# Four moves in the TensorE order of a fused attention and FFN kernel, and one move on ScalarE

## The chip, the cores and the metric

The kernel runs on one core of a Trainium2 chip. The metric is device time in microseconds (us) for one execution, the median of several. The core has five engines that run side by side and meet only at semaphores: TensorE (PE in the profile, its weight loads PEld), VectorE (DVE), ScalarE (ACT), GpSimd (POOL) and SyncE (SP), which here issues the DMAs.

## The reference

For each of 8 batches of 128 tokens and 512 features the program computes an attention block and an FFN block, each with a residual.

```python
c  = x @ cond_weight[id1].T                  # a weight chosen per batch
q, k, v = c @ Wq, c @ Wk, c @ Wv             # 32 query heads, 8 key/value groups, head size 16
q, k = rope(q), rope(k)
w  = softmax(causal(q k^T) / 4)
x1 = x + (w v) @ Wo
h  = x1 @ W.T + 0.5 * (x1 @ lora_A[id2]) @ lora_B.T
out = x1 + h @ W_base.T + b_base + 2 * sum_top2( gate_e * (h @ A_e^T) @ B_e^T )   # router: h @ W_router.T
```

## The kernel before

**Tiling.** A batch is one tile of 128 tokens. All fp32 products are made from two rounded parts ("hi" and "lo"): `with_high` adds hi times hi and lo times hi for the four slices of 128 features (8 matmuls), `with_low` the four others. ScalarE makes a hi part (a copy), VectorE the lo part (a difference), so a product over a fresh tile waits first for ScalarE and then for VectorE. The FFN's weights are fused ahead of the loop: `fused_w` holds W times [router, experts' A, W_base], cut into a left block (`HALF` = 324 columns: 8 router logits, 128 expert values, 188 base columns) and a right block. The rank part (x1 times lora_A, rank 32) is `project_low`, four matmuls into `d_ps`; `split_low` on ScalarE and VectorE makes `low_t` from it, and one matmul with `lora_g` (line 1141, "the last product") adds it to a block.

**Rounds.** The work is a software pipeline. Round t (1 to 6) holds batch f = t + 1 (condition, q, k, v, first scores), batch t (maxima, transposed scores, exponentials), batch r = t - 1 (context, output projection, x1, FFN) and batch q = t - 2 (experts, output). Before the rounds stands a prologue, behind them a tail that finishes batches 6 and 7.

**What sets the order.** Each engine's order is written out by hand as a list of calls, and each engine executes its list in order. Nothing is reordered by a scheduler; a wait at the head of the list holds everything behind it on that engine.

**The steps that matter here, by engine:**
- TensorE: `transpose_maxima` (line 1013) turns the row maxima of batch t; `score_t(t, e)` makes the transposed scores of one half e: 16 mask products of 32x32 (line 1025, "the mask"), 12 products (line 1030, "the passes"), 4 that subtract the maxima (line 1035). `project_out` (lines 976, 977, 981) makes the attention output of batch r. `transpose_qk` (lines 1096 and 987) turns q and k of batch f; `transpose_x1` (line 987) turns x1; `project_low` (line 1126); `project_ffn` (lines 976, 977, 981, then 1141); `score(f, 0)` and `score(f, 1)` (line 1003). The last product of the left block signals `gates_done`.
- ScalarE: `copy_v` (v out of PSUM), `spread_maxima` (four copies into `max_rows`), `split_context`, `exp_scores` (line 519), `split_qk`, `split_x1`, `split_low`.
- VectorE: `choose_experts` starts on `gates_done` (line 794), then `add_x_base`, `maxima` 0, `gate_hidden`, `maxima` 1, `turn_context` (line 703), `split_hidden`, `split_c` (line 622, `c_t_lo`), `maxima` 2 and 3, `split_maxima`, context scaling, `add_out`, the rotations (lines 735, 737), `split_context`, `add_x` (line 775) and the lo parts.
- GpSimd: `add_rotated` (line 374) makes the rotated k and q for `transpose_qk`; `split_a` (line 369).

Of the kernel before, what the change touches and what calls it, by code (L numbers as in the profile page):

```python
# [19 lines left out]
def build_program(nc, x, x_t, cond_ids, lora_ids, cond_w_t, w_q, w_kv, w_o, cos, sin, w2, lora_a, lora_b,  # L20
# [34 lines left out]
    with ExitStack() as ctx:  # L55
# [361 lines left out]
        def _(act):  # L417
# [78 lines left out]
            def copy_v(f):  # L496
                act.wait_ge(kv_done, f + 1)
                if f == 0:
                    act.wait_ge(zeroed, 9)
                v = d_ps[:, KV:2 * KV].rearrange("s (j e d) -> s j e d", e=2, d=HD)  # L500
                for e in range(2):
                    copy(v_ones[f % 2][e][:, :, 0, :], v[:, :, e, :]).then_inc(v_ready, 1)
# [67 lines left out]
            for t in ROUNDS:  # L570
# [10 lines left out]
                if prep:  # L581
                    split_condition(g, range(KT))
                    split_xt(g)
                if batch(f):
                    copy_v(f)
                if batch(t):
# [3 lines left out]
                if batch(t):  # L590
                    exp_scores(t, 0)
                if batch(f):
                    split_qk(f)
                if batch(r):
# [25 lines left out]
        def _(dve):  # L620
# [352 lines left out]
        def _(pe):  # L973
# [41 lines left out]

            def score_t(t, e):
                if e == 0:
                    pe.wait_ge(maxed, HEADS * (t + 1))
                    if t == 0:
                        pe.wait_ge(owns_made, 7)  # L1020
                for j in range(PAIRS):
                    if e == 1:
                        pe.wait_ge(exped, 8 * t + j + 1)
                    for b in range(PAIRS):
                        nc.tensor.matmul(s_ps[j][tile_rows(b), :], ident_b[tile_rows(j), tile_rows(j)],
                                         later_b[tile_rows(j), b, :].unsqueeze(1).broadcast_to([TILE, PER, P]),
                                         start=True, stop=False)
                for key, query in passes(k_pad[t % 2], q_t[t % 2]):
                    for j in range(PAIRS):
                        nc.tensor.matmul(s_ps[j][:, :], key[tile_rows(j), e, :], query[tile_rows(j), :, :],  # L1030
                                         start=False, stop=False)
                if e == 0:
                    pe.wait_ge(max_spread, t + 1)
# [53 lines left out]

            def project_kv(f):
                if f > 1:
                    pe.wait_ge(ctx_turned, 2 * (f - 1))  # L1090
                with_high(d_ps[:, 0:2 * KV], c_t, qkv_w, slice(D, QKV))
                with_low(d_ps[:, 0:2 * KV], c_t, qkv_w, slice(D, QKV)).then_inc(kv_done, 1)
# [6 lines left out]
            def project_out(r):  # L1099
                pe.wait_ge(o_lo, KT)  # L1100
                pe.wait_ge(ctx_hi, r + 1)
# [4 lines left out]
                elif r > 0:  # L1106
                    pe.wait_ge(out_ready, r)
                with_high(attn_ps(r)[:, :], ctx_t, o_w, slice(0, D))
                pe.wait_ge(ctx_lo, r + 1)
                with_low(attn_ps(r)[:, :], ctx_t, o_w, slice(0, D)).then_inc(attn_done, 1)  # L1110
# [18 lines left out]

            def project_ffn(r, n, to, part=slice(0, HALF)):  # L1130
                cols = slice(n * HALF + part.start, n * HALF + part.stop)
                if r == 0:
# [3 lines left out]
                if n == 0 and r == LAST - 1:  # L1136
                    pe.wait_ge(ctx_turned, 2 * r + 3)
                with_high(to[:, part], x1_t, fused_w, cols)
                with_low(to[:, part], x1_t, fused_w, cols, last=False)
                pe.wait_ge(low_lo, r + 1)  # L1140
                return nc.tensor.matmul(to[:, part], low_t, lora_g[:, cols], start=False, stop=(n == 0))

            def transpose_hidden(q):
# [73 lines left out]
            for t in ROUNDS:  # L1217
# [20 lines left out]
                if batch(f):  # L1238
                    project_kv(f)
                if batch(t):  # L1240
                    transpose_maxima(t)
                    score_t(t, 0)
# [92 lines left out]
```

## Time and profile before

| | |
|---|---|
| median of 3 runs | 255.9 us (255.59 to 256.31) |
| profiled execution, device time | 255.72 us |
| its span in the profile | 253.9 us |
| TensorE busy | 228.1 us (90%) |
| VectorE busy | 182.6 us (72%) |
| ScalarE busy | 117.3 us (46%) |
| GpSimd busy | 86.5 us (34%) |

The span runs from the first to the last instruction; 1.8 us of the execution lie outside it. A matmul's end in the profile is modelled and overlaps the next one's start, so TensorE is read by the starts of its rows: two full rows of 512 columns start 0.23 us apart. TensorE's granted clock is full in nearly all slices.

### The profile page before, as it was taken

Reading aid. Unit: us, or ns where it says so; the run is one execution under the profiler, and the core shown is the slowest. Engines: PE = TensorE matmul, PEld = TensorE weight load, DVE = VectorE, ACT = ScalarE, POOL = GpSimd, SP = SyncE. Lnnn points to the kernel's source line nnn. Section 1 sums busy time; section 2 is a strip of 40 time slices with the busy share of each in tenths; the row PEclk is TensorE's granted clock in tenths of the full one; section 3 lists DMA queues with packets and bytes.
Section 4 is the critical chain, followed back from the end, with each engine's and each line's share of the span. In section 5 each row is a group of like instructions: output and inputs, shape, how many; then the busy total and the mean of one; then the engine's idle time right before and its main releaser. Section 6 shows DMA issues by size and latency. Waiting matters only on the chain.

```text
span 253.9 us, 5663 instructions
## 1 busy us (share of the span) xinstructions
PE 228.1 (90%) x1978; PEld 169.9 (67%) x1978; DVE 182.6 (72%) x915; ACT 117.3 (46%) x269; POOL 86.5 (34%) x93
## 2 busy tenths in 40 slices
PE   0588999989999999999999998999999998989894
PEld 0477977765667676777667766867775764656793
DVE  3499367638966896599749974988488947967753
ACT  3596436477374237514661566066602461054210
POOL 7200562359178006900490039202930140002020
PEclk9999999999999999999999999999999999999998
DMA  5999208015002401250116011601100120001111
GB/s 118 335 381 366 98 7 252 4 27 183 12 5 79 170 1 52 54 196 4 52 44 206 4 53 41 209 1 54 41 3 0 45 52 0 3 1 55 41 41 41
DMA packets 20047, 21.16 MB, mean 83 GB/s; under 512 B 6452, under 2 KB 11572, under 8 KB 20020
## 3 DMA queue, kind: packets, MB, share of 16 engines
q1 hardware_dynamic: 20020, 20.81, 25.3%
q8 instruction: 15, 0.25, 0.4%
q14 instruction: 12, 0.10, 0.1%
HBM read 18.71 MB, written 2.10 MB: 82 GB/s over the span
## 4 chain that ended last, share of the span: by engine, by line
PE 66%; DVE 16%; ACT 11%; issue 3%; DMA 1%; SPq 1%; POOL 1%; DVEq 0%
PE bank L976 10%; PE bank L981 9%; PE bank L977 9%; ACT stage_d L519 5%; PE bank L1055 5%; PE bank L1003 4%; PE bank L1069 3%; PE bank L987 3%; PE bank L1030 3%; DVE thrown L685 3%; PE bank L1071 3%; PE bank L1070 3%; ACT max_rows L419 2%; PE bank L1035 2%; DVE x L775 2%
## 5 line engine op out<-in xcount | busy, mean ns | idle before, releaser
L685 DVE CUSTOM_DVE_ANT_0 thrown<-bank,causal 128x128 f32<-128x128 f32 x256 | 56.1, 285 | 0.0
L374 POOL TENSOR_TENSOR rope_b<-rope_a,rope_b 128x128 f32<-128x128 f32 (+1 forms) x16 | 16.3, 1016 | 94.5 <-DVE rope_b L737 94.5
L354 POOL TENSOR_TENSOR cond_w_lo<-cond_raw,cond_w_hi 128x512 fp32r<-128x512 f32 x28 | 35.2, 1287 | 23.9 <-ACT cond_w_hi L419 23.9
L1069 PE MATMUL bank<-cond_w_hi,xt_hi 128*128 128x512 f32 x32 | 13.6, 425 | 9.4 <-DVE cond_w_lo L622 9.4
L976 PE MATMUL bank<-qkv_w_hi,c_t_hi 128*128 128x512 f32 (+1 forms) x64 | 21.4, 352 | 0.6 <-DVE c_t_lo L622 0.5
L685 DVE DVE_READ_ACCUMULATOR2_ANT neg_max<- 128x1 f32 x256 | 21.0, 82 | 0.0
L976 PE MATMUL bank<-fused_w_hi,late 128*128 128x324 f32 (+2 forms) x68 | 20.5, 316 | 0.0
L977 PE MATMUL bank<-qkv_w_lo,c_t_hi 128*128 128x512 f32 (+1 forms) x64 | 20.5, 337 | 0.0
L383 POOL TENSOR_TENSOR x_bias<-x,bias_row 128x512 f32<-128x512 f32 x8 | 10.2, 1277 | 29.9 <-DVE out_sb L843 28.8
L977 PE MATMUL bank<-fused_w_lo,late 128*128 128x324 f32 (+2 forms) x68 | 19.9, 306 | 0.0
L419 ACT ACTIVATE cond_w_hi<-cond_raw 128x512 fp32r<-128x512 f32 x32 | 17.9, 623 | 3.8 <-DMA cond_raw<-cond_w_t 3.8
L519 ACT ACTIVATE stage_d<-bank 128x512 f32<-128x512 f32 x32 | 16.5, 605 | 6.4 <-PE bank L1035 6.3
L419 ACT ACTIVATE v_ones<-bank 128x64 f32<-128x64 f32 x16 | 2.7, 221 | 32.0 <-PE bank L981 32.0
L419 ACT ACTIVATE turn<-bank 128x512 f32<-128x512 f32 x8 | 4.8, 597 | 27.2 <-PE bank L1071 27.2
L976 PEld LDWEIGHTS bank<-qkv_w_hi,c_t_hi 128*128 128x128 f32 x64 | 12.0, 188 | 7.8 <-issue 4.3
L519 ACT ACTIVATE stage_a<-bank 128x512 f32<-128x512 f32 x32 | 16.5, 604 | 1.4 <-PE bank L1035 0.6
L419 ACT ACTIVATE late<-bank 128x128 fp32r<-128x128 f32 (+1 forms) x24 | 9.5, 396 | 15.4 <-PE bank L1147 10.4
L775 DVE TENSOR_TENSOR x<-bank,x_nat 128x512 f32<-128x512 f32 x8 | 5.5, 691 | 12.2 <-PE bank L981 12.2
L976 PE MATMUL bank<-shared,late 128*128 128x512 f32 x32 | 13.1, 408 | 1.1 <-issue 0.7
L703 DVE STREAM_TRANSPOSE turned<-bank 128x512 f32<-128x512 f32 x16 | 11.4, 712 | 3.5 <-PE bank L1055 3.4
L419 ACT ACTIVATE max_rows<-bank,own_p 128x128 fp32r<-128x128 f32 x32 | 9.1, 378 | 10.2 <-PE bank L1013 10.1
L981 PE MATMUL bank<-qkv_w_hi,c_t_lo 128*128 128x512 f32 (+1 forms) x64 | 13.8, 337 | 0.0
(151 smaller groups left out, 619.6 us busy)
## 6 DMA issues: line engine op xcount, KB each, us to landing
cond_raw<-cond_w_t SPq DMA_DIRECT2D x7, 1024.0 KB, 5.6
xt_raw<-x_t SPq DMA_DIRECT2D x8, 256.0 KB, 5.9
x_nat<-x SPq DMA_DIRECT2D x8, 256.0 KB, 2.7
out<-out_sb SPq DMA_DIRECT2D x8, 256.0 KB, 2.0
cond_raw<-cond_w_t SPq DMA_DIRECT2D x4, 256.0 KB, 3.6
stage_d<-base_t SPq DMA_DIRECT2D x4, 256.0 KB, 5.8
stage_b<-w SPq DMA_DIRECT2D x4, 256.0 KB, 6.5
stage_a<-w_q SPq DMA_DIRECT2D x4, 256.0 KB, 6.5
```

The costliest lines, as they stand in the source:

```text
L354: pool.tensor_tensor(cond_w.lo[:, k, :], cond_raw[:, k, :], f32(cond_w.hi[:, k, :]), ALU.subtract).then_inc(cond_lo, 1)
L374: pool.tensor_tensor(qk[:, at:at + w], rope_a[:, at:at + w], rope_b[:, at:at + w], ALU.add).then_inc(qk_ready, 1)
L419: return nc.scalar.activation(out, in_, ACT.Copy, scale=scale)
L519: nc.scalar.activation(probs_t[e][j], s_ps[j][:, :], ACT.Exp).then_inc(exped, 1)
L685: nc.vector.tensor_tensor_reduce(thrown[:, p % 2, j, e, :], s_ps[j][:, at:at + P], causal[:, :], -1.0, -MASKED, ALU.add, ALU.min, neg_max[ ...
L703: nc.vector.transpose(turned[e][:, :, :, :].rearrange("q b s d -> q (b s d)"), ctx_ps(r, e)[:, :]).then_inc(ctx_turned, 1)
L775: nc.vector.tensor_tensor(x1[:, :], attn_ps(r)[:, :], x_nat[:, :], ALU.add).then_inc(x1_ready, 1)
L976: nc.tensor.matmul(out, lhs.hi[:, k, :], rhs.hi[:, k, cols], start=(k == 0), stop=False)
L977: nc.tensor.matmul(out, lhs.hi[:, k, :], rhs.lo[:, k, cols], start=False, stop=False)
L981: mm = nc.tensor.matmul(out, lhs.lo[:, k, :], rhs.hi[:, k, cols], start=False, stop=(last and k == KT - 1))
L1055: mm = nc.tensor.matmul(ctx_ps(r, e)[tile_rows(j), :], v_ones[r % 2][e][:, j, :, :], probs_t[e][j], start=True, stop=True)
L1069: nc.tensor.matmul(y_ps[:, :], xt.hi[:, k, :], cond_w.hi[:, k, :], start=(k == 0), stop=False)
```

## The change

It moves work in the rounds; nothing is added to or taken from the computation.
1. ScalarE: `copy_v` goes from ahead of `spread_maxima` to behind `exp_scores(t, 0)`. It now also waits for `rope_k`; `rotate_k` on VectorE waits for `kv_done` in place of `v_ready`, and `transpose_qk` waits for `v_ready`.
2. TensorE: `transpose_maxima` goes between the 8 high and the 4 low products of keys and values.
3. TensorE: the mask of the second half goes ahead of `transpose_x1`.
4. TensorE: `project_low` goes behind the 12 products of the left block, which now wait for `x1t_hi` and `x1t_lo` separately.
5. TensorE: the left block's last product, which signals `gates_done`, goes behind `score(f, 0)` and `score(f, 1)`.

```diff
@@ ScalarE, rounds
-                if batch(f):
-                    copy_v(f)
                 if batch(t):
                     spread_maxima(t)
                 if batch(r):
                     split_context(r)
                 if batch(t):
                     exp_scores(t, 0)
                 if batch(f):
+                    copy_v(f)
                     split_qk(f)
@@ copy_v, rotate_k, transpose_qk
                 act.wait_ge(kv_done, f + 1)
+                if f > 1:
+                    act.wait_ge(rope_k, f + 1)
...
-                dve.wait_ge(v_ready, 2 * (f + 1))
+                if f < 2:
+                    dve.wait_ge(v_ready, 2 * (f + 1))
+                else:
+                    dve.wait_ge(kv_done, f + 1)
...
                 pe.wait_ge(qk_ready, 2 * (f + 1))
+                pe.wait_ge(v_ready, 2 * (f + 1))
@@ TensorE, rounds
                 if batch(f):
-                    project_kv(f)
+                    project_kv_high(f)
                 if batch(t):
                     transpose_maxima(t)
+                if batch(f):
+                    project_kv_low(f)
+                if batch(t):
                     score_t(t, 0)
                 if batch(r):
                     project_out(r)
                 if batch(f):
                     transpose_qk(f)
+                if batch(t):
+                    mask_t(t, 1)
                 if batch(r):
                     transpose_x1(r)
                 if batch(t):
-                    score_t(t, 1)
-                if batch(r):
+                    passes_t(t, 1)
+                    less_maxima(t, 1)
+                if batch(r):
+                    ffn_high(r, 0, left_ps(r))
+                    ffn_low_half(r, 0, left_ps(r))
                     project_low(r)
-                    project_ffn(r, 0, left_ps(r)).then_inc(gates_done, 1)
                 if batch(f):
                     score(f, 0)
                     score(f, 1)
+                if batch(r):
+                    ffn_rank(r, 0, left_ps(r)).then_inc(gates_done, 1)
                 if batch(r) and f < LAST:
                     project_ffn(r, 1, right_ps(r))
```

On TensorE in a round, before: from the k and q transposes to the first block product. `rope_b` holds the rotated q and k, `x` is the tile x1, `late` a region that holds x1's parts.

```order
L1096 MATMUL bank<-ident,rope_b 128x128
L987 MATMUL bank<-ident,rope_b 128x128 x4
L987 MATMUL bank<-ident,x 128x128 x4
L1025 MATMUL bank<-later_b,ident_b 32x512 x16
L1030 MATMUL bank<-q_t_hi,k_pad_hi 128x512 x4
```

The same place in the changed kernel, as it is printed with the semaphores that are waited for (the mask in its first four products and the fifth):

```order
L1117 MATMUL bank<-ident,rope_b 128x128 [waits v_ready,qk_ready]
L992 MATMUL bank<-ident,rope_b 128x128 x4
L1035 MATMUL bank<-later_b,ident_b 32x512 [waits exped]
L1035 MATMUL bank<-later_b,ident_b 32x512 x3
...
L992 MATMUL bank<-ident,x 128x128 [waits x1_ready]
L992 MATMUL bank<-ident,x 128x128 x3
L1042 MATMUL bank<-q_t_hi,k_pad_hi 128x512 x4
```

The mask stood behind x1's transposes and now stands between them and q's.

On TensorE before, from the subtraction of the maxima to the next scores; `late` at line 1126 is x1 and lora_A, `lora_g` the last product's weight.

```order
L1035 MATMUL bank<-max_rows,pick_max 128x512 x4
L1126 MATMUL bank<-late 128x256 [waits x1t_lo,a_lo,x1t_hi,k_lo]
L1126 MATMUL bank<-late 128x256 x3
L976 MATMUL bank<-fused_w_hi,late 128x324
...
L981 MATMUL bank<-fused_w_hi,late 128x324 x4
L1141 MATMUL bank<-lora_g,late 128x324 [waits low_lo]
L1003 MATMUL bank<-k_pad_hi,q_t_hi 128x256 [waits exped,q_lo,k_lo]
```

And in the changed kernel:

```order
L1049 MATMUL bank<-max_rows,pick_max 128x512 x4
L981 MATMUL bank<-fused_w_hi,late 128x324 [waits x1t_hi]
...
L986 MATMUL bank<-fused_w_hi,late 128x324 [waits x1t_lo]
L986 MATMUL bank<-fused_w_hi,late 128x324 x3
L1153 MATMUL bank<-late 128x256 [waits x1t_lo,a_lo,x1t_hi,k_lo]
L1153 MATMUL bank<-late 128x256 x3
L1008 MATMUL bank<-k_pad_hi,q_t_hi 128x256 [waits exped,q_lo,k_lo]
...
L1179 MATMUL bank<-lora_g,late 128x324 [waits low_lo]
L981 MATMUL bank<-fused_w_hi,late 128x324 [waits x1t_hi]
```

The rank part moved behind twelve products, and the last product behind the 24 of the scores.

On ScalarE, before, and then in the changed kernel; `v_ones` is v, `stage_a` takes the exponentials of the first half.

```order
L419 ACTIVATE v_ones<-bank 128x4x16 [waits kv_done]
L419 ACTIVATE v_ones<-bank 128x4x16
L419 ACTIVATE max_rows<-bank,own_p 128x128 [waits max_t,scored_t]
L419 ACTIVATE max_rows<-bank,own_p 128x128 x3
L419 ACTIVATE late<-stage_d 128x512 [waits ctx_normed]
```

```order
L419 ACTIVATE max_rows<-bank,own_p 128x128 [waits max_t,scored_t]
L419 ACTIVATE max_rows<-bank,own_p 128x128 x3
L419 ACTIVATE late<-stage_d 128x512 [waits ctx_normed]
L521 ACTIVATE stage_a<-bank 128x512 [waits scored_t,ctx_done]
L521 ACTIVATE stage_a<-bank 128x512 [waits scored_t] x3
L419 ACTIVATE v_ones<-bank 128x4x16 [waits rope_k,kv_done]
```

The copies of v moved from the head of this piece to its end.

## Rows read from the trace of the kernel before

**Rows 1.** The page's part 4, the chain that ended last, by engine.

```profile
PE 66%; DVE 16%; ACT 11%; issue 3%; DMA 1%; SPq 1%; POOL 1%; DVEq 0%
```

**Rows 2.** Timeline (start us, us, operation, [idle before <-releaser]): the last gates of the rounds, and the tail.

```profile
211.30 0.30 DVE L794 COPY gates<-bank 128x136 f32<-128x136 f32 x1 [0.51 <-PE bank L1141]
...
216.18 0.39 PE L1003 MATMUL bank<-k_pad_hi,q_t_hi 32*128 32x256 f32 x4 [1.07 <-DVE neg_max L685]
```

**Rows 3.** Timeline of TensorE, round 3, second half of the round.

```profile
122.73 0.19 PEld L1035 LDWEIGHTS bank<-max_rows,pick_max 32*128 32x128 f32 x4 [0.52 <-ACT max_rows L419]
...
126.13 0.27 PE L1096 MATMUL bank<-ident,rope_b 128*128 128x128 f32 x1
...
127.07 0.66 PE L987 MATMUL bank<-ident,x 128*128 128x128 f32 x4 [0.24 <-DVE x L775]
...
127.66 0.43 PE L1025 MATMUL bank<-later_b,ident_b 32*32 32x512 bf16 x16
...
128.03 0.50 PE L1030 MATMUL bank<-q_t_hi,k_pad_hi 32*128 32x512 f32 x4
...
128.82 0.41 PE L1035 MATMUL bank<-max_rows,pick_max 32*128 32x512 f32 x4
...
129.45 0.71 PE L1126 MATMUL bank<-late 128*128 128x256 f32 x4 [0.22 <-DVE late L622]
...
130.00 0.31 PE L976 MATMUL bank<-fused_w_hi,late 128*128 128x324 f32 x1
...
131.19 0.76 PE L981 MATMUL bank<-fused_w_hi,late 128*128 128x324 f32 x4
...
132.24 0.42 PE L1141 MATMUL bank<-lora_g,late 128*128 128x324 f32 x1 [0.29 <-DVE late L788]
...
132.59 0.39 PE L1003 MATMUL bank<-k_pad_hi,q_t_hi 32*128 32x256 f32 x4
...
133.50 0.41 PE L976 MATMUL bank<-fused_w_hi,late 128*128 128x324 f32 x1
```

**Rows 4.** Timeline of ScalarE, round 3: exponentials of the second half, then the rank part.

```profile
129.31 2.07 ACT L519 ACTIVATE stage_d<-bank 128x512 f32<-128x512 f32 x4 [0.84 <-PE bank L1035]
...
131.23 0.31 ACT L419 ACTIVATE late<-bank 128x128 fp32r<-128x128 f32 x1
```

**Rows 5.** Timeline of VectorE: round 3, then the head of round 6.

```profile
106.56 0.30 DVE L794 COPY gates<-bank 128x136 f32<-128x136 f32 x1 [0.51 <-PE bank L1141]
...
113.38 0.72 DVE L703 STREAM_TRANSPOSE turned<-bank 128x512 f32<-128x512 f32 x1
...
114.68 0.69 DVE L622 TENSOR_TENSOR c_t_lo<-bank,c_t_hi 128x512 fp32r<-128x512 f32 x1 [0.41 <-ACT c_t_hi L419]
...
123.52 0.74 DVE L737 TENSOR_TENSOR rope_b<-bank,rope_sin 128x256 f32<-128x256 f32 x2
...
185.17 0.30 DVE L794 COPY gates<-bank 128x136 f32<-128x136 f32 x1 [0.51 <-PE bank L1141]
...
191.98 0.72 DVE L703 STREAM_TRANSPOSE turned<-bank 128x512 f32<-128x512 f32 x1 [0.37 <-PE bank L1055]
```

**Rows 6.** Timeline of GpSimd, round 3: the addition that completes the rotated q.

```profile
124.34 1.66 POOL L374 TENSOR_TENSOR rope_b<-rope_a,rope_b 128x512 f32<-128x512 f32 x1 [0.81 <-DVE rope_b L737]
```

**Rows 7.** Timeline of TensorE: maxima's transpose in round 1, and two rows of the tail.

```profile
68.81 0.33 PE L1013 MATMUL bank<-ident,max_cols 128*128 128x128 f32 x1 [0.54 <-DVE max_cols L695]
...
228.47 0.41 PE L1035 MATMUL bank<-max_rows,pick_max 32*128 32x512 f32 x4
228.81 1.06 PE L1055 MATMUL bank<-stage_a,v_ones 128*32 128x512 f32 x8
```

**Rows 8.** Timeline: one small VectorE operation in two rounds, and GpSimd's `split_a`.

```profile
107.17 0.60 DVE L800 TENSOR_SCALAR top_less<-top,neg_top 128x2 f32<-128x2 f32 x1
...
107.28 0.45 POOL L369 TENSOR_TENSOR late<-a_raw,late 128x128 fp32r<-128x128 f32 x1
...
185.78 0.23 DVE L800 TENSOR_SCALAR top_less<-top,neg_top 128x2 f32<-128x2 f32 x1
```

More of the change, by code:

```diff
@@ L1016, in score_t, with mask_t @@
             def score_t(t, e):
+                mask_t(t, e)
+                passes_t(t, e)
+                less_maxima(t, e)
+            def mask_t(t, e):
                 if e == 0:
@@ L1027, in score_t, with passes_t @@
                                          start=True, stop=False)
+            def passes_t(t, e):
                 for key, query in passes(k_pad[t % 2], q_t[t % 2]):
@@ L1031, in score_t, with less_maxima @@
                                          start=False, stop=False)
+            def less_maxima(t, e):
                 if e == 0:
@@ L1088, in project_kv, with project_kv_high @@
             def project_kv(f):
+                project_kv_high(f)
+                project_kv_low(f)
+            def project_kv_high(f):
                 if f > 1:
@@ L1091, in project_kv, with project_kv_low @@
                 with_high(d_ps[:, 0:2 * KV], c_t, qkv_w, slice(D, QKV))
+            def project_kv_low(f):
                 with_low(d_ps[:, 0:2 * KV], c_t, qkv_w, slice(D, QKV)).then_inc(kv_done, 1)
@@ L1099, in project_out, with project_out_high @@
             def project_out(r):
+                project_out_high(r)
+                project_out_low(r)
+            def project_out_high(r):
                 pe.wait_ge(o_lo, KT)
@@ L1108, in project_out, with project_out_low @@
                 with_high(attn_ps(r)[:, :], ctx_t, o_w, slice(0, D))
+            def project_out_low(r):
                 pe.wait_ge(ctx_lo, r + 1)
@@ L1128, in project_low, with ffn_high @@
                 mm.then_inc(low_done, 1)
-            def project_ffn(r, n, to, part=slice(0, HALF)):
-                cols = slice(n * HALF + part.start, n * HALF + part.stop)
+            def ffn_high(r, n, to, part=slice(0, HALF)):
                 if r == 0:
@@ L1137, in project_ffn, with ffn_low, ffn_low_half, ffn_rank @@
                     pe.wait_ge(ctx_turned, 2 * r + 3)
-                with_high(to[:, part], x1_t, fused_w, cols)
+                pe.wait_ge(x1t_hi, r + 1)
+                with_high(to[:, part], x1_t, fused_w, slice(n * HALF + part.start, n * HALF + part.stop))
+            def ffn_low(r, n, to, part=slice(0, HALF)):
+                ffn_low_half(r, n, to, part)
+                return ffn_rank(r, n, to, part)
+            def ffn_low_half(r, n, to, part=slice(0, HALF)):
+                cols = slice(n * HALF + part.start, n * HALF + part.stop)
+                pe.wait_ge(x1t_lo, r + 1)
                 with_low(to[:, part], x1_t, fused_w, cols, last=False)
+            def ffn_rank(r, n, to, part=slice(0, HALF)):
+                cols = slice(n * HALF + part.start, n * HALF + part.stop)
                 pe.wait_ge(low_lo, r + 1)
                 return nc.tensor.matmul(to[:, part], low_t, lora_g[:, cols], start=False, stop=(n == 0))
+            def project_ffn(r, n, to, part=slice(0, HALF)):
+                ffn_high(r, n, to, part)
+                return ffn_low(r, n, to, part)
             def transpose_hidden(q):
@@ L1238, in _ @@
                 if batch(f):
-                    project_kv(f)
+                    project_kv_high(f)
                 if batch(t):
                     transpose_maxima(t)
+                if batch(f):
+                    project_kv_low(f)
+                if batch(t):
                     score_t(t, 0)
```

## The prediction

> **What bounds the kernel now.** I read the page first: TensorE is busy 90% of the span, and the chain that ended last runs for 66% on TensorE, 16% on VectorE and 11% on ScalarE [rows 1]. So nearly all is TensorE, broken by short trips to other engines. Next I read the timeline of one round by TensorE's starts. The reader is to see four places where TensorE stands though its weights could be loaded. (a) The subtraction of the maxima starts at 122.73, held by `max_rows`: the weight load stood 0.52 us for ScalarE. (b) After the k and q transposes (126.13) x1's start only at 127.07. Five transposes take about 0.69 (x1's four take 127.66 - 127.07 = 0.59 to the next operation, plus one of 0.1), so 0.25 us are waited for x1, as its own row says (0.24). (c) `project_low` starts 0.63 after line 1035 (128.82 to 129.45), where the tail has 0.34 for the same step without a wait (228.47 to 228.81) [rows 7]: 0.29 us. (d) The last product of the left block starts at 132.24. The four low products began at 131.19, 0.15 each, so it could have been at 131.79: 0.45 us, for `low_t` [rows 3]. In all about 1.5 us in a round.
>
> A round lasts 26.18 us: gates start at 106.56 [rows 5] and, four rounds later, at 211.30 [rows 2].
>
> Then I asked whether VectorE could follow a faster TensorE. Its head of a round starts at the gates and runs without a gap to the first context transpose: 113.38 - 106.56 = 6.82 us in round 3, and in round 6, less the idle 0.37, 191.98 - 0.37 - 185.17 = 6.44 [rows 5]. In the tail it is already the bound: TensorE stands 1.07 us for the maxima of batch 7 [rows 2].
>
> **The change, part by part.**
>
> *Moves 1 and 2 (v copied later, maxima turned earlier).* (a) goes away on TensorE: two copies of v no longer stand ahead of `spread_maxima`, and the turned maxima come four products earlier. Cost: TensorE's four low products of k and v are now queued behind a wait for `split_maxima`. In round 1 that wait was 0.54 us even at the old place [rows 7]; there the gain of (a) is lost again. The copies of v now stand behind 2 us of exponentials, but the q and k transposes that wait for them come after the whole output projection (12 products of 0.23 = 2.8 us) and still wait for GpSimd's sum of the rotated q, which ended at 126.00 (124.34 + 1.66) [rows 6], only 0.13 us ahead of TensorE's 126.13 [rows 3]. So I price v at nothing; without that cover it would be its two copies, some 0.3 us. But here stands the limit: whatever TensorE gains ahead of the transposes beyond 0.13 us, it waits for GpSimd, whose sum hangs on VectorE's rotations.
>
> *VectorE's chain, which then sets the time of the transposes.* From the gates: head 6.63 (middle of 6.44 and 6.82). Context transpose to `c_t_lo`, without its idle time: 114.68 - 0.41 - 113.38 = 0.89. From there to the end of the q rotation, one queue without a wait on TensorE: 123.52 + 0.74 - 114.68 = 9.58. To the end of GpSimd's sum: 126.00 - 124.26 = 1.74. Handover: between 0 and 0.13, taken as 0.06. Sum 18.90 us after the gates, where round 3 had 126.13 - 106.56 = 19.57 [rows 3, 5, 6].
>
> *Move 3 (mask ahead of x1's transposes).* It fills (b). The mask takes 0.37 among its like (127.66 to 128.03); between full-size transposes I take 0.45, an estimate with one more switch of tile shape. Order after the transposes start at 0: q and k 0.69, mask 0.45, x1 0.59, passes 0.79 (128.03 to 128.82), so line 1035 at 2.52; it was at 2.69. The wait is replaced by the mask, and only 0.17 is won [rows 3].
>
> *Move 4 (rank part behind the block).* (c) goes: the 12 products need only x1's hi part, then its lo part. They start at 2.52 + 0.34 = 2.86 and take 12 x 0.149 = 1.79 (eight in 131.19 - 130.00), so `project_low` starts at 4.65 and ends, with its 0.71, at 5.36. ScalarE's `split_low` could start at 5.40. Before it started at 131.23 - 126.13 = 5.10, right behind the exponentials [rows 3, 4]. So `low_t`, which is wanted for the gates, comes 0.30 us later than before, counted from the transposes.
>
> *Move 5 (last product behind the scores).* The scores start at 4.65 + 0.46 = 5.1, when the exponentials (2.52 + 0.49 + 2.07 = 5.08) are just done, and take 0.91 (132.59 to 133.50): until 6.0. `low_t` is ready 6.41 after the transposes (132.24 - 126.13 = 6.11, plus 0.30). So the wait (d) is covered by the scores save 0.4 us, and the last product is at 6.41, the gates 0.45 later at 6.86, where they were at 6.56 (132.24 + 0.45) [rows 3, 4].
>
> *Sum.* A round becomes 18.90 + 6.86 = 25.76 us instead of 26.18: 0.42 us less. TensorE by itself could have shortened it by more (the block to the right starts right behind the scores), but VectorE starts its head 0.3 later against the transposes, so TensorE will wait where it did not: some 0.3 us at `score(t, 2)` for the maxima, 0.2 at the output projection or the transposes. Between the gates of round 1 and those of round 6 lie five rounds: 2.1 us. Round 1 itself has no saving ahead of its transposes and pays the 0.30. The tail starts with VectorE's queue on the gates of round 6 and TensorE waits for it there [rows 2]; it moves as a whole. In all 2.1 - 0.3 = 1.8 us: 255.72 - 1.8 = **253.9 us**, against the profiled execution, which lies 0.2 under the median of 255.9.
>
> *A rule that speaks against it.* One small VectorE operation at the head, line 800, takes 0.23 us in round 6 and 0.60 in round 3, where GpSimd's `split_a` (107.28 to 107.73) lies over it [rows 8]. The gates will come at another moment of GpSimd's work, so this can hit in any round; that is the 6.44 and the 6.82 above. By the rows, a hit in every round costs 0.19 x 5 = 0.95 us more (254.9), none saves as much (252.9). The Trainium skill, page SBUF — State Buffer, section "Who interferes with whom", says that some VectorE operations and GpSimd share a port pair, that it is an exclusive lock and that the one that comes second is blocked for the whole instruction. The row agrees: the operation ended just after `split_a` did.
>
> **The rivals.**
> *A, a larger gain.* `low_t` is not later (the mask and the block pack more tightly than I added), and the head is the short one: 25.76 - 0.30 - 0.19 = 25.27 a round, 0.91 saved, 4.6 in five, nothing lost in round 1: 251.2 us. For it: each of my TensorE steps is taken from rows with drains in them. Against it: the order makes `project_low` wait for 1.79 us of products. Chance 0.22.
> *B, TensorE's waits simply vanish:* 1.5 x 6 = 9 us, 246.7. It needs a VectorE chain that can shrink, and this one has idle time only at two places of 0.4 [rows 5]. Chance 0.07.
> *C, no change.* Each e us that the gates come later after the transposes than my 6.86 costs 6e (five rounds and round 1), so 1.8 us are gone at e = 0.30. If the block starts 0.63 behind line 1035, as `project_low` did, instead of 0.34, e is 0.29: 255.6 us. For it: that 0.63 may be a cost of the step and not a wait. Chance 0.14.
> *D, slower.* The same mechanism further on: the last product is queued behind 24 score products, and these behind the exponentials. From e = 0.43 it is slower by 0.8. The scores' end at 6.0 has 0.4 of room before it moves the gates; if the exponentials or q's lo part hold the scores by 0.85 us, e is 0.45 and the time 255.72 + 0.9 = 256.6 us. Against it: q's lo part was ready long before the scores. Chance 0.09.
>
> **How the numbers follow.** My forecast, 253.9, has a chance of 0.48 with its own range 252.9 to 254.9. A measurement of this kernel tells some 0.3% (0.8 us) from no change. Faster: forecast, A and B, 0.77. Within 0.3%: C, 0.14. Slower: D, 0.09. The range takes in most of A and of C: 251.2 to 255.7, and leaves B, D and the edges out.
>
> **What the profile after would show.** Right: rounds 25.8 us apart by their gates; no idle time of the maxima's subtraction (a); the mask between q's and x1's transposes and no wait of x1's; `low_t`'s split on ScalarE now released by TensorE and not by its own queue; no idle on VectorE before the first context transpose; TensorE waiting at `score(t, 2)` for `maxed`, and for GpSimd's sum. Wrong: a VectorE with idle time at its head as before (then TensorE still leads and A or B holds), or gates more than 7.1 us behind the transposes (C or D). The whole would fall if v or the maxima made a new wait of over 0.5 us in each round.

## The result and the profile after

The changed kernel takes 252.44 us (median of four runs, 252.13 to 252.94) where the kernel before, on the same chip, takes 256.11 (255.59 to 256.52): a ratio of 0.986, with a 95% interval from 0.983 to 0.989. It is faster by 3.7 us; I had said 1.8.

| | before | after |
|---|---|---|
| profiled execution, device time | 255.72 us | 252.94 us |
| span | 253.9 us | 251.2 us |
| TensorE, VectorE busy | 90%, 72% | 91%, 72% |
| start of the gates, rounds 1 and 6 | 80.41, 211.30 | 81.19, 208.52 |
| distance of rounds (mean of five, gates to gates) | 26.18 us | 25.47 us |
| from the last gates of the rounds to the end | 42.65 us | 42.65 us |

The chain that ended last, by engine; it answers to [rows 1].

```profile
PE 62%; DVE 26%; issue 5%; ACT 3%; DMA 1%; SPq 1%; POOL 1%; DVEq 0%
```

VectorE's share went from 16% to 26% and ScalarE's from 11% to 3%. The work of both is nearly the same, so this is no longer the same loop: the kernel now ends where VectorE's queue lets it. The timeline of VectorE in round 3, by its queue, shows it; it answers to [rows 5].

```profile
106.49 0.30 DVE L799 COPY gates<-bank 128x136 f32<-128x136 f32 x1 [0.52 <-PE bank L1179]
...
107.10 0.47 DVE L805 TENSOR_SCALAR top_less<-top,neg_top 128x2 f32<-128x2 f32 x1
...
113.05 0.71 DVE L704 STREAM_TRANSPOSE turned<-bank 128x512 f32<-128x512 f32 x1
...
113.86 0.68 DVE L623 TENSOR_TENSOR c_t_lo<-bank,c_t_hi 128x512 fp32r<-128x512 f32 x1
...
122.69 0.74 DVE L738 TENSOR_TENSOR rope_b<-bank,rope_sin 128x256 f32<-128x256 f32 x2
...
130.89 0.28 DVE L790 SCALAR_TENSOR_TENSOR low_rest<-bank,late 32x128 f32<-32x128 f32 x1 [1.93 <-ACT late L419]
...
131.99 0.30 DVE L799 COPY gates<-bank 128x136 f32<-128x136 f32 x1 [0.51 <-PE bank L1179]
```

From the gates to the q rotation (106.49 to 123.43) no row carries idle time. `c_t_lo`, which waited 0.41 us for ScalarE in [rows 5], waits no longer. Then the chain leaves VectorE: GpSimd adds the rotated q, and TensorE takes it. GpSimd's timeline, against [rows 6], and then TensorE's, against [rows 3]:

```profile
123.50 1.67 POOL L374 TENSOR_TENSOR rope_b<-rope_a,rope_b 128x512 f32<-128x512 f32 x1 [0.80 <-DVE rope_b L738]
```

```profile
113.19 0.39 PE L1008 MATMUL bank<-k_pad_hi,q_t_hi 32*128 32x256 f32 x4 [0.36 <-DVE neg_max L686]
...
121.72 0.41 PE L1049 MATMUL bank<-max_rows,pick_max 32*128 32x512 f32 x4
...
124.07 1.19 PE L986 MATMUL bank<-shared,late 128*128 128x512 f32 x4
125.23 0.33 PE L1117 MATMUL bank<-ident,rope_b 128*128 128x128 f32 x1
125.40 0.60 PE L992 MATMUL bank<-ident,rope_b 128*128 128x128 f32 x4
125.93 0.43 PE L1035 MATMUL bank<-later_b,ident_b 32*32 32x512 bf16 x16
126.29 0.66 PE L992 MATMUL bank<-ident,x 128*128 128x128 f32 x4
...
127.67 0.41 PE L1049 MATMUL bank<-max_rows,pick_max 32*128 32x512 f32 x4
128.01 0.42 PE L981 MATMUL bank<-fused_w_hi,late 128*128 128x324 f32 x1
...
129.91 0.64 PE L1153 MATMUL bank<-late 128*128 128x256 f32 x4
130.47 0.39 PE L1008 MATMUL bank<-k_pad_hi,q_t_hi 32*128 32x256 f32 x4
...
131.54 0.41 PE L1179 MATMUL bank<-lora_g,late 128*128 128x324 f32 x1
```

Three of the prediction's four places are without a wait: the subtraction of the maxima (121.72), x1's transposes (126.29) and the first block product (128.01). Of the fourth, the wait for `low_t`, a rest of 0.16 us is left: the scores take 0.91 from 130.47, so the last product could start at 131.38, and it starts at 131.54. TensorE waits elsewhere too: 0.36 us at `score(t, 2)` for the maxima, and at the q transposes. Four products of 0.23 from 124.07 would have let them start at 124.99; they start at 125.23, 0.06 behind the end of GpSimd's sum (125.17). ScalarE's row for `low_t`, against [rows 4], is released by TensorE, as foreseen:

```profile
130.58 0.28 ACT L419 ACTIVATE late<-bank 128x128 fp32r<-128x128 f32 x1 [0.35 <-PE bank L1153]
```

### The profile page after: what moved, and what is told of

The parts are those of the page before. It is cut to its first block, busy times and chain, and to the rows that moved or that the text cites. A ratio compares the mean times of both kernels' runs of the same rounds, so it can differ in the third digit from the quotient of the medians.

```text
span 251.2 us, 5681 instructions
## 1 busy us (share of the span) xinstructions
PE 227.5 (91%) x1978; PEld 170.1 (68%) x1978; DVE 181.9 (72%) x915; ACT 117.9 (47%) x269; POOL 86.6 (34%) x93
## 3 DMA queue, kind: packets, MB, share of 16 engines
HBM read 18.71 MB, written 2.10 MB: 83 GB/s over the span
## 4 chain that ended last, share of the span: by engine, by line
PE 62%; DVE 26%; issue 5%; ACT 3%; DMA 1%; SPq 1%; POOL 1%; DVEq 0%
PE bank L981 11%; PE bank L986 10%; PE bank L982 9%; DVE thrown L686 8%; PE bank L1042 5%; PE bank L992 3%; PE bank L1069 3%; PE bank L1008 3%; PE bank L1035 2%; PE bank L1083 2%; PE bank L1049 2%; PE bank L1084 1%; PE bank L1179 1%; PE bank L1153 1%; DMA cond_raw<-cond_w_t 1%
## 5 line engine op out<-in xcount | busy, mean ns | idle before, releaser
L981 PEld LDWEIGHTS bank<-fused_w_hi,late 128*128 128x128 f32 x68 | 12.8, 188 | 2.3 <-ACT late L419 1.8
L1083 PEld LDWEIGHTS bank<-cond_w_hi,xt_hi 128*128 128x128 f32 x32 | 6.5, 204 | 10.9 <-issue 9.6
L1008 PE MATMUL bank<-k_pad_hi,q_t_hi 32*128 32x256 f32 x128 | 10.9, 328 | 3.2 <-DVE neg_max L686 2.9
```

Source lines behind the costliest of these rows:

```text
L981: nc.tensor.matmul(out, lhs.hi[:, k, :], rhs.hi[:, k, cols], start=(k == 0), stop=False)
L1008: mm = nc.tensor.matmul(s_ps[j][:, at:at + 2 * P], query[tile_rows(j), p, :], key[tile_rows(j), :, :], start=(n == 0), stop=(n == 2))
L1083: nc.tensor.matmul(y_ps[:, :], xt.hi[:, k, :], cond_w.hi[:, k, :], start=(k == 0), stop=False)
```

## The experiments

Each ratio is against the kernel before, measured beside it, with its 95% interval. "Distance" is that of the gates from round to round, (start in round 6 less start in round 1) / 5. "From gates 1" is the span behind the first gates; it leaves out the prologue, whose length differs from execution to execution (the first gates lie between 80.15 and 82.57). In the three kernels that put maxima ahead of the gates the gates themselves start later against all else, so there this last column can't be held against the others, only among the three.

| kernel | median us | ratio | distance us | from gates 1, us |
|---|---|---|---|---|
| before | 255.9 | 1 | 26.18 | 173.5 |
| after | 252.4 | 0.986 (0.983 to 0.989) | 25.47 | 170.0 |
| undo5 | 256.5 | 1.003 (1.001 to 1.005) | 26.27 | 174.0 |
| undo4 | 254.3 | 0.993 (0.991 to 0.996) | 25.69 | 171.1 |
| undo3 | 253.4 | 0.990 (0.987 to 0.992) | 25.48 | 170.0 |
| undo12 | 252.8 | 0.988 (0.986 to 0.990) | 25.52 | 170.3 |
| pad_after | 255.3 | 0.998 (0.996 to 0.999) | 26.04 | 172.9 |
| pad_before | 256.2 | 1.001 (0.999 to 1.002) | 26.18 | 173.5 |
| max_first | 250.7 | 0.979 (0.977 to 0.981) | 25.15 | 166.9 |
| only5 | 254.7 | 0.995 (0.993 to 0.997) | 25.81 | 171.7 |
| only45 | 253.7 | 0.990 (0.988 to 0.992) | 25.72 | 171.3 |
| right_late_before | 256.7 | 1.003 (1.001 to 1.006) | 26.23 | 173.8 |
| right_late_best | 252.5 | 0.986 (0.983 to 0.989) | 25.45 | 168.4 |
| hidden_late | 250.3 | 0.976 (0.973 to 0.980) | 25.01 | 166.2 |

**Which of the moves brings it.** Four kernels each undo one move in the changed kernel. `undo5` puts the last product ahead of the scores again:

```diff
                     project_low(r)
+                    ffn_rank(r, 0, left_ps(r)).then_inc(gates_done, 1)
                 if batch(f):
                     score(f, 0)
                     score(f, 1)
-                if batch(r):
-                    ffn_rank(r, 0, left_ps(r)).then_inc(gates_done, 1)
```

> The changed kernel with move 5 undone: the left block's last product stands ahead of the scores again, behind the rank part. Theory (VectorE's queue from the gates to the q rotation, GpSimd's sum and TensorE's stretch from the transposes to the gates make a round of 25.5 us, and TensorE has some 0.4 us to spare ahead of VectorE): the gates keep their 6.8 us behind the transposes, but TensorE reaches the next condition 1.0 us later, so that TensorE leads again at the head; a round becomes 26.1 us, VectorE idles before the context transpose, time 255.0 to 256.0 us, nearly all of the gain lost. Rival (each move is worth its own removed wait in the same proportion, additively, 3.4 us shared out by 0.49, 0.24, 0.29 and 0.45): 253.5 us.

Measured: 256.46 us, a distance of 26.27: 0.5 us above the range that I had given. The whole gain is gone, and a little more; the rival's 253.5 is excluded. TensorE's timeline in round 3:

```profile
133.09 0.42 PE L1179 MATMUL bank<-lora_g,late 128*128 128x324 f32 x1 [1.00 <-DVE late L793]
133.44 0.39 PE L1008 MATMUL bank<-k_pad_hi,q_t_hi 32*128 32x256 f32 x4
...
136.38 0.40 PE L1083 MATMUL bank<-cond_w_hi,xt_hi 128*128 128x512 f32 x1
```

The 0.29 us that this product's row shows in [rows 3] became 1.00 us, because the rank part is later, and no work of the scores lies over it. The gates themselves are not later for it: the last product starts 6.31 us behind the q transposes (126.78 to 133.09), exactly as in the kernel after (125.23 to 131.54), since `low_t` releases it in both.

`undo4` puts `project_low(r)` ahead of the block again, and leaves the scores ahead of the last product.

```diff
                 if batch(r):
+                    project_low(r)
                     ffn_high(r, 0, left_ps(r))
                     ffn_low_half(r, 0, left_ps(r))
-                    project_low(r)
```

> The changed kernel with move 4 undone: the rank part ahead of the left block's products, the last product still behind the scores. Theory: TensorE waits again 0.3 to 0.5 us for x1's lo part at the rank part, and the last product now stands behind block and scores, at 6.65 us after the transposes instead of 6.3; the gates come 0.33 us later in each of six rounds: 254.4 us (253.8 to 255.2). Rival (additive shares): 253.1 us.

Measured: 254.30 us, a distance of 25.69: 0.22 more a round. TensorE's timeline shows the wait (c) back, and larger: TensorE comes there sooner, now that the mask fills wait (b), while x1's parts are no earlier (the row starts 3.39 us behind the transposes, 3.32 in [rows 3]).

```profile
129.55 0.71 PE L1153 MATMUL bank<-late 128*128 128x256 f32 x4 [0.54 <-DVE late L623]
```

The gates come 7.18 us behind the q transposes, 0.42 later than after (6.76), but only 0.22 reaches the round. VectorE gives the rest back, as its timeline shows: line 805 takes 0.23 us here and 0.47 after, and the head is 6.32 against 6.56.

```profile
107.66 0.30 DVE L799 COPY gates<-bank 128x136 f32<-128x136 f32 x1 [1.36 <-PE bank L1179]
...
108.26 0.23 DVE L805 TENSOR_SCALAR top_less<-top,neg_top 128x2 f32<-128x2 f32 x1
...
113.98 0.71 DVE L704 STREAM_TRANSPOSE turned<-bank 128x512 f32<-128x512 f32 x1
```

`undo3` and `undo12` take back the mask's place, and moves 1 and 2 together.

```diff
                     transpose_qk(f)
-                if batch(t):
-                    mask_t(t, 1)
                 if batch(r):
                     transpose_x1(r)
                 if batch(t):
+                    mask_t(t, 1)
                     passes_t(t, 1)
```

> The changed kernel with move 3 undone: the mask behind x1's transposes. Theory: x1 is now ready 0.8 us after the first transpose of q and k, only 0.1 us after TensorE could start on it, so the order costs 0.12 us a round: 253.1 us (252.4 to 253.5). Rival (the wait of 0.24 us for x1 returns whole): 253.9 us or more.

```diff
@@ ScalarE
+                if batch(f):
+                    copy_v(f)
                 if batch(t):
                     spread_maxima(t)
...
                 if batch(f):
-                    copy_v(f)
                     split_qk(f)
@@ TensorE
                 if batch(f):
-                    project_kv_high(f)
+                    project_kv(f)
                 if batch(t):
                     transpose_maxima(t)
-                if batch(f):
-                    project_kv_low(f)
-                if batch(t):
                     score_t(t, 0)
```

The waits of `copy_v` and `rotate_k` are those of the kernel before there.

> The changed kernel with moves 1 and 2 undone: v's copies ahead of the spread of the maxima, maxima's transpose behind the four low products of k and v. Theory: TensorE waits 0.5 us for the spread of the maxima, but GpSimd's sum releases the transposes anyway, so that only 0.15 to 0.25 us of it reach the round: 253.4 us (252.7 to 253.9). Rival (the wait of 0.49 us counts whole in six rounds): 255.4 us.

Measured: 253.38 and 252.75 us, distances of 25.48 and 25.52. Neither is told apart from the changed kernel by its rounds (25.47). `undo12` falls short of the 253.4 expected: the wait (a) is back ahead of the output projection, and TensorE, which waits for GpSimd's sum behind that projection, had room for about half of it. In round 3 its q transposes start 0.22 behind GpSimd's sum (125.38 to 125.60), where it was 0.06; VectorE's shorter head (6.45 against 6.56) and a shorter way from the transposes to the gates (6.70 against 6.76) give that back. In `undo3` the way from the q transposes to the gates is 6.90 us against 6.76 (126.06 to 132.96), as expected, but VectorE's head is 6.43 against 6.56, so nearly all of it is given back. The timeline of GpSimd in that kernel, and then that of VectorE, shows why:

```profile
107.91 0.47 POOL L369 TENSOR_TENSOR late<-a_raw,late 128x128 fp32r<-128x128 f32 x1
```

```profile
107.46 0.30 DVE L799 COPY gates<-bank 128x136 f32<-128x136 f32 x1 [0.51 <-PE bank L1179]
...
108.06 0.34 DVE L805 TENSOR_SCALAR top_less<-top,neg_top 128x2 f32<-128x2 f32 x1
```

`split_a` ends at 108.38 there and line 805 at 108.40: it takes 0.34 us, and 0.47 in the kernel after, where `split_a` lies over it for longer.

**Moves alone, from the other side.** `only5` is the kernel before with move 5 alone, `only45` with moves 4 and 5.

```diff
                     project_low(r)
-                    project_ffn(r, 0, left_ps(r)).then_inc(gates_done, 1)
+                    ffn_but_rank(r, 0, left_ps(r))
                 if batch(f):
                     score(f, 0)
                     score(f, 1)
+                if batch(r):
+                    ffn_rank(r, 0, left_ps(r)).then_inc(gates_done, 1)
```

> The kernel before with move 5 alone: the left block's last product behind the scores, the rank part where it was. Theory: TensorE gains 0.45 us a round, but the gates come 0.5 us later after the transposes, and VectorE's queue leads: rounds of 25.8 us, 254.6 us (254.0 to 255.3). Rival (the moves are worth their own waits): 254.9 us or less with VectorE still idle ahead of its context transpose.

```diff
                 if batch(r):
+                    ffn_high(r, 0, left_ps(r))
+                    ffn_low_half(r, 0, left_ps(r))
                     project_low(r)
-                    project_ffn(r, 0, left_ps(r)).then_inc(gates_done, 1)
                 if batch(f):
                     score(f, 0)
                     score(f, 1)
+                if batch(r):
+                    ffn_rank(r, 0, left_ps(r)).then_inc(gates_done, 1)
```

> The kernel before with moves 4 and 5 alone (in other words the changed kernel with moves 1, 2 and 3 undone together). Theory: moves 1 to 3 save time on TensorE ahead of a point that GpSimd's sum releases, and TensorE has 0.6 us to spare there in the changed kernel; without them the 0.5 us wait for the spread of the maxima is absorbed, and the later mask costs 0.0 to 0.15 us a round: 252.4 to 253.6 us. Rival (the three are worth their share when undone together, since either covers for the other): 254 us or more.

Measured: 254.66 us, as expected, and 253.67. By the distances, move 5 alone is worth 0.37 us a round, move 4 behind it 0.09 more (the medians are 1.0 us apart, of which five times 0.09 is about half), moves 1 to 3 together the other 0.25 (25.72 to 25.47). By the medians alone that last step isn't clear: the intervals of `only45` and of the kernel after overlap a little. `only45` came out 0.07 over the upper end that the theory gave: I had held moves 1 to 3 for worth nothing, since each alone is. Together they are worth something. TensorE's waits in `only45`, summed over the run (us in total, times, longest):

```profile
PE bank L988 <- DVE x L776: 2.1, 7, 0.7
```

This is wait (b), 0.7 us in sum in the changed kernel. The traces show where the 0.25 lies. From the gates to the q transposes the two kernels need the same in the mean of the five rounds (18.71 and 18.70). From the transposes to the gates `only45` needs 7.01 and the changed kernel 6.77, and nearly all of that stands ahead of the subtraction of the maxima: 2.69 us behind the transposes against 2.44. Taking back move 3 alone costs 0.13 there (126.06 to 128.63 is 2.57), because GpSimd's sum holds the transposes until 1.16 us after the four low products of the projection began, and x1 is nearly ready when they end. In `only45` TensorE comes to them later than GpSimd's sum, 0.91 behind those products, and waits 0.24 for x1. So wait (b) costs 0.25 where wait (a) stands too, and half of that where it doesn't.

**Is VectorE's queue the bound now?** Two small memsets on unused rows stand between the first maxima and `gate_hidden`, once in the kernel after, once in the kernel before.

```diff
                 if batch(q):
+                    nc.vector.memset(low_rest[64:96, :], 0.0)
+                    nc.vector.memset(low_rest[96:128, :], 0.0)
                     gate_hidden(q)
```

> The changed kernel with two small memsets of 128 columns more on VectorE, between the first and the second maxima of rounds 2 to 6 (they write rows of a scratch tile that nothing reads, 0.3 to 0.4 us together). Theory (VectorE's queue sets the round): each round grows by the whole of it, five times: 254.0 to 254.5 us. Rival (TensorE sets the round): under 0.3 us more, 252.4 to 252.7 us.

> The kernel before with the same two memsets. Theory: in the kernel before VectorE idled 0.2 to 0.4 us ahead of the context transpose and 0.4 us ahead of c's lo part, so that the memsets vanish there: 255.9 to 256.4 us, no more than 0.3 us above the kernel before. Rival (VectorE's queue set the round before as well): 1.5 to 2 us more.

Measured: 255.31 us after, with 0.57 more a round, and 256.20 before, with none (26.18). In the kernel before they are covered: `c_t_lo`, which waits for c, starts 8.12 us behind the gates with them (106.98 to 115.10) and without them (106.56 to 114.68). In the kernel after each microsecond of VectorE ahead of the first context transpose is paid in full: 7.15 us from the gates to that transpose (106.01 to 113.16) instead of 6.56. The memsets themselves cost more than I had taken. VectorE's timeline of `pad_after`, from the last of the first eight maxima, and then the same place in the kernel after:

```profile
109.31 0.08 DVE L686 DVE_READ_ACCUMULATOR2_ANT neg_max<- 128x1 f32 x1
109.47 0.17 DVE L898 MEMSET low_rest<- 32x128 f32 x1
109.70 0.17 DVE L899 MEMSET low_rest<- 32x128 f32 x1
109.88 0.15 DVE L819 TENSOR_REDUCE top_sum<-top_exp 128x1 f32<-128x2 f32 x1
...
113.16 0.71 DVE L704 STREAM_TRANSPOSE turned<-bank 128x512 f32<-128x512 f32 x1
```

```profile
109.78 0.08 DVE L686 DVE_READ_ACCUMULATOR2_ANT neg_max<- 128x1 f32 x1
109.78 0.15 DVE L819 TENSOR_REDUCE top_sum<-top_exp 128x1 f32<-128x2 f32 x1
```

Line 819 starts together with that last row in the kernel after, and 0.57 us behind it in `pad_after`.

**A version from it.** If VectorE's queue behind the gates is the bound, work that needs no gates should stand ahead of them. `max_first` does that with the first eight row maxima; the experts' `gate_hidden` then follows the choice at once (the tail is changed likewise).

```diff
+                if batch(t):
+                    maxima(t, 0)
                 if batch(q):
                     choose_experts(q)
                     add_x_base(q)
-                if batch(t):
-                    maxima(t, 0)
-                if batch(q):
                     gate_hidden(q)
```

> The changed kernel with the first group of maxima ahead of the choice of experts on VectorE, in rounds 2 to 6 and in the tail; the hidden values of the experts are gated right behind the choice. Theory: VectorE needn't wait for the gates to begin its queue (it idles 0.5 us there); the queue begins 0.5 us earlier, and TensorE can follow: rounds of 25.0 us, 249.4 to 250.2 us. Rival (TensorE is nearly the bound already): under 1 us gained, 251.5 us or more.

Measured: 250.74 us, a ratio of 0.979 to before. That is above the 249.4 to 250.2 expected. The time from TensorE's transposes to `c_t_lo` is now set by TensorE: `c_t_lo` waits for c, as it did in the kernel before. The loop through c closes: 6.31 us from the q transposes to the last product, 2.17 to the condition, 4.02 to c's transposes, 1.27 to `c_t_lo`, 9.59 and 1.74 to GpSimd's sum and 0.05 to the next q transposes are 25.15, the distance measured. The timeline of VectorE in `max_first`:

```profile
107.52 0.29 DVE L799 COPY gates<-bank 128x136 f32<-128x136 f32 x1
...
112.13 0.71 DVE L704 STREAM_TRANSPOSE turned<-bank 128x512 f32<-128x512 f32 x1
...
113.21 0.69 DVE L623 TENSOR_TENSOR c_t_lo<-bank,c_t_hi 128x512 fp32r<-128x512 f32 x1 [0.19 <-ACT c_t_hi L419]
```

The gates carry no idle time any more, and `c_t_lo` does. So what delays c counts next: the right block, 13 products between the last product and the next condition. Two kernels move it behind c's transposes, in the kernel before and in `max_first`.

```diff
                     transpose_c(f)
+                if batch(q):
+                    project_ffn(q, 1, right_ps(q))
...
-                if batch(r) and f < LAST:
-                    project_ffn(r, 1, right_ps(r))
```

> The kernel before with the right block's products moved from the end of a round to the next round, behind the transposes of c, so that the condition begins 1.9 us earlier. Theory (in the kernel before TensorE's own queue with its four waits closes at 26.2 us, and none of the four waits is touched): 255.6 to 256.6 us, no gain, though VectorE no longer idles ahead of c's lo part. Rival (what move 5 gained is only that the condition and c's lo part come earlier): 252.5 us or less.

> The kernel with the first maxima ahead of the choice of experts (250.7 us), and the right block's products moved behind the transposes of c in the next round. Theory: there VectorE idles 0.2 us for c's hi part in each round, since the condition stands behind the right block; that goes away, 0.2 us a round: 249.5 us (249.0 to 250.2). Rival (TensorE's queue is the bound by now): 250.7 us or more.

Measured: 256.72 and 252.54 us. The first lies 0.1 above the range given, the second missed its range, and there the rival's number holds. In the kernel before nothing is gained, so c's way was not its only bound. By its rows that loop closes at 26.00 us: 6.11 from the q transposes to the last product, 3.29 to the condition, 4.01 to c's transposes, 1.27 to `c_t_lo`, 9.58 and 1.74 as in the prediction. A round took 26.18; what set it in the end was TensorE's own queue with its waits, 0.13 behind GpSimd's sum. Moving a block within that queue doesn't shorten it. In `max_first` it was slower by 1.8 us, where I expected 1.2 less. TensorE's timeline:

```profile
109.55 1.07 PE L1068 MATMUL bank<-stage_a,v_ones 128*32 128x512 f32 x8
111.08 0.33 PE L1188 MATMUL bank<-ident,hidden 128*128 128x128 f32 x1 [0.46 <-DVE hidden L834]
111.24 0.60 PE L991 MATMUL bank<-ident,turn 128*128 128x128 f32 x4
```

With the right block gone from its head, TensorE comes to the transpose of the experts' hidden values before VectorE has made them, and c's transposes are queued behind it. I had followed c and not what stands ahead of it. `hidden_late` mends that place:

```diff
@@ TensorE
-                if batch(q):
-                    transpose_hidden(q)
                 if batch(f):
                     transpose_c(f)
                 if batch(q):
+                    transpose_hidden(q)
                     project_ffn(q, 1, right_ps(q))
@@ ScalarE, VectorE
+                if batch(f):
+                    split_c(f)
                 if batch(q):
                     split_hidden(q)
-                if batch(f):
-                    split_c(f)
```

> The kernel of right_late_best (first maxima ahead of the choice of experts; right block's products behind c's transposes) with the transpose of the experts' hidden values moved behind c's transposes too, and on ScalarE and VectorE the hi and lo parts of c ahead of those of the hidden values. Theory: TensorE's wait of 0.46 us a round for the hidden values ahead of c's transposes, which made right_late_best 1.8 us slower than max_first, goes away; a round goes from 25.45 to about 25.0 us, where VectorE's own queue (24.95 us) is the next bound: 249.9 us, from 249.4 to 250.6. Rival: the right block's new place costs by itself, because what was moved there lies in a part of the round in which TensorE's queue is already full: 252 us or more.

Measured: 250.30 us, a ratio of 0.976 to before, a distance of 25.01, so it was what stood ahead of c's transposes and not the right block's new place, and the rival falls. (The kernel also splits c ahead of the hidden values on ScalarE and VectorE; the two were not separated.) It is the lowest of all, but against `max_first` (0.979) the intervals of the ratios overlap; in the traces its rounds are 0.14 us shorter. TensorE's timeline at the q transposes, and GpSimd's ahead of them:

```profile
123.44 1.08 PE L985 MATMUL bank<-shared,late 128*128 128x512 f32 x4
124.36 0.27 PE L1116 MATMUL bank<-ident,rope_b 128*128 128x128 f32 x1
```

```profile
122.41 1.68 POOL L374 TENSOR_TENSOR rope_b<-rope_a,rope_b 128x512 f32<-128x512 f32 x1 [0.80 <-DVE rope_b L738]
```

The transposes follow the projection's four products (4 x 0.23 = 0.92) without a gap, 0.27 us behind GpSimd's sum (124.09): at this place TensorE leads again, and not VectorE's queue, as I had expected of this kernel.

## Why the prediction was right in kind and too small in size

**The total.** The measured 252.44 lies inside my range of 251.2 to 255.7, but under the likeliest case's own range of 252.9 to 254.9; it is nearer to rival A's 251.2 than to my 253.9. That the range holds it is owed in part to the range's width. In the traces, five rounds are shorter by 3.56 us (130.89 to 127.33); I had said 2.1. Round 1 is longer by 0.19 (from the condition of batch 2 to the gates 23.61 us, and 23.42 before); I had said 0.30. The tail moved as a whole, as said. Sum: 3.37 us less by the mechanism, and in this execution 0.59 more in the prologue, which no move touches (the condition starts at 57.58 and 56.99). -3.37 + 0.59 = -2.78, which is 252.94 - 255.72.

**The steps.** The mis-sized step is "a round becomes 18.90 + 6.86 = 25.76 us". It measured 18.74 + 6.76 = 25.50 in round 3:

| term | forecast | after, round 3 |
|---|---|---|
| gates to first context transpose | 6.63 | 6.56 |
| to `c_t_lo` | 0.89 | 0.81 |
| to the end of the q rotation | 9.58 | 9.57 |
| to the end of GpSimd's sum | 1.74 | 1.74 |
| handover | 0.06 | 0.06 |
| transposes to line 1049 | 2.52 | 2.44 |
| to the first block product | 0.34 | 0.34 |
| to the last product | 3.55 | 3.53 |
| to the gates | 0.45 | 0.45 |

The loop is the one that I named, and no term is off by 0.1; but three errors of 0.07 to 0.08 point the same way and are paid five times. They are the estimate of 0.45 for the mask (0.36), the head, and the way to `c_t_lo`, from which I had taken off only the idle time that its row shows. The remaining 0.03 is the mean of the rounds (25.47) against round 3.

The head was misread and not only taken too long. In the kernel before, the context transpose starts 6.81 or 6.82 us behind the gates in each of the five rounds, though line 800 takes anything from 0.23 to 0.60 in them: TensorE's context released it, in round 3 too, after a wait of 0.05 that is too short to be printed. So 6.82 was TensorE's time and not the queue's, and the middle of it and 6.44 had no meaning. The queue by itself needs 6.32 with line 805 at 0.23 (`undo4`), and 6.56 with 0.47.

Another term was off and did no harm: I gave the rank part's four products 0.46 us until the scores start, and they took 0.56 (129.91 to 130.47). The last product is released by `low_t` and not by the scores, so the sum did not feel it.

**The chance given to the rivals.** A (251.2) was right that things pack more tightly, and wrong on `low_t`: its split on ScalarE is at 5.35 us behind the transposes against 5.10, so 0.25 later (I had said 0.30). C fell, since the first block product stood 0.34 behind line 1049, so the 0.63 of before was a wait. B fell, since TensorE's waits moved in part to `score(t, 2)` and the q transposes; and D, since the scores ended before `low_t` was there.

**What my account of the moves had wrong.** I told the gain as four waits that go away, and priced move 5 as a cover for one of them. `undo5` shows that it carries the change: without it the time is 256.5. The wait for `low_t` is covered by the scores, so the gates are no later, and the scores no longer stand between the gates and the next condition. So c comes 1.1 us earlier against the gates: the condition stood 3.3 us behind line 1179 in `undo5` (133.09 to 136.38), and stands 2.2 behind it after, in TensorE's timeline:

```profile
106.03 0.42 PE L1179 MATMUL bank<-lora_g,late 128*128 128x324 f32 x1
...
108.21 0.40 PE L1083 MATMUL bank<-cond_w_hi,xt_hi 128*128 128x512 f32 x1
```

That is why `c_t_lo` lost its 0.41 of idle time. I had subtracted that idle time without saying what takes it away. Moves 1 and 2, which I put first, are not seen alone.

**The rule on the shared port.** Line 805 took 0.47 us in round 3 with `split_a` (107.07 to 107.54) over it, ended 0.03 after it, and took 0.34 in `undo3` and 0.23 in `max_first`. So this hit costs up to 0.24 us in these kernels (0.37 in [rows 8]) and varies with the moment, and the head passes it on whole: 6.32, 6.43 and 6.56 us for 0.23, 0.34 and 0.47. I had priced it at 0.19 a round by the two heads. In the kernel after it is there in rounds 3 to 6 (0.47 to 0.49), which last 25.50 to 25.53 us, and nearly absent in round 2 (0.25), which lasts 25.30. The rounds were shorter than forecast all the same. The Trainium skill, page SBUF — State Buffer, section "Who interferes with whom", tells of an exclusive lock between VectorE and GpSimd; the ends of the rows agree with it.

## What to carry to other kernels

Find each loop from one round to the next, and not only the waits: here two closed within 0.2 us of one another (TensorE's own queue, and VectorE by GpSimd back to TensorE), so a wait removed from one is worth at most that difference until the other is shortened too. The last instruction whose result others wait for should stand behind work that covers its own wait and ahead of work that nobody waits for; where the moved work goes, read what is queued in front of the next critical instruction (`right_late_best`). When a bound is a queue, the test is cheap: pad it by half a microsecond, and look whether the round grows by as much.

## What the runs showed of the hardware that I had not expected

- The mask, 16 products of 32x32 tiles, costs 0.36 us between full-size transposes (125.93 to 126.29) where it cost 0.37 between x1's transposes and the passes (127.66 to 128.03): no further price of the change of shape shows at this place. Elsewhere there may be one: from the subtraction of the maxima to the full-size product behind it the step is 0.34 (127.67 to 128.01).
- A memset of 32x128 has a row of 0.17 us, but two of them lengthen the round by 0.57 us. The first starts 0.16 behind the row ahead of it, with which line 819 starts at once where no memset stands between; the second starts 0.23 later, and line 819 0.18 after that (109.31, 109.47, 109.70, 109.88).
- A single VectorE operation on 128x2 values (line 805, 800 before) takes from 0.23 to 0.60 us. In the rounds read, wherever it took over 0.23, it ended 0.02 to 0.04 us after GpSimd's `split_a`.
